# A batch's projections end 6 slots ahead of its scores in place of 24, and the order of tiles, roots, packs and loads around them changes

## The reference, cut to what matters

```python
def _rmsnorm(t):
    return t * jax.lax.rsqrt(jnp.mean(t * t, axis=-1, keepdims=True) + EPS)
q = x @ Wq.T                       # x: layer norm of the block's input
k_raw = context @ Wk.T
v_raw = context @ Wv.T
...
q = _rmsnorm(q)
k = _rmsnorm(k)
scores = jnp.einsum('bhnd,bhmd->bhnm', q, k) * scale
attn = jax.nn.softmax(scores, axis=-1)
out = jnp.einsum('bhnm,bhmd->bhnd', attn, v)
...
x = x + jnp.tanh(g_xattn[0]) * _L0_xattn_ref(_layernorm(x, axis=-1), ctx_2048, L0_xattn_Wq, L0_xattn_Wk, L0_xattn_Wv)
x = x + jnp.tanh(g_ffn[0]) * _L0_ffn_ref(_layernorm(x, axis=-1), L0_ffn_router_w, ...)
```

## Time and profile before

| what | value |
|---|---|
| median of 3 runs | 1108.07 us (1106.4 to 1108.37) |
| the profiled execution: its time | 1103.48 us |
| its span | 1101.4 us |
| TensorE busy | 1047.0 us, 95% of the span |
| VectorE busy | 603.8 us, 55% |
| ScalarE busy | 568.7 us, 52% |
| GpSimd busy | 169.3 us, 15% |
| mean granted clock of TensorE | 0.977 |

### The profile page before, as it was taken

One profiled execution on the slowest core, in us unless ns is written; L12 is line 12 of the kernel. 1 busy time (PEld: TensorE's weight loads), 2 busy tenths in 40 slices (PEclk: granted clock), 3 DMA queues, 4 the chain that ended last, 5 costly groups with the idle time before them and its releaser, 6 DMA issues. The chain is left out here.

```text
span 1101.4 us, 26510 instructions
## 1 busy us (share of the span) xinstructions
PE 1047.0 (95%) x11645; PEld 852.4 (77%) x11645; DVE 603.8 (55%) x1187; ACT 568.7 (52%) x862; POOL 169.3 (15%) x170
## 2 busy tenths in 40 slices
PE   4889999999999999999669999999999999999997
PEld 3667777777777777776458788888888999999996
DVE  4774455644446554553447644434447666666663
ACT  4356766766676676667543221212125555555552
POOL 0000111101111111111322220000011212333111
PEclk9999999999999999999669999999999999999999
DMA  7400000000000000000113120101038777787762
GB/s 231 104 8 29 30 29 29 30 20 11 29 30 29 29 29 29 2 2 2 43 32 126 50 69 20 39 20 36 15 119 247 233 219 232 231 233 221 214 206 77
DMA packets 62170, 93.14 MB, mean 85 GB/s; under 512 B 5378, under 2 KB 43266, under 8 KB 62048
## 3 DMA queue, kind: packets, MB, share of 16 engines
q1 hardware_dynamic: 53544, 74.90, 22.4%
q0 software_dynamic: 5664, 13.18, 3.9%
q10 hardware_dynamic: 2840, 3.29, 1.0%
HBM read 82.24 MB, written 10.29 MB: 84 GB/s over the span
## 5 line engine op out<-in xcount | busy, mean ns | idle before, releaser
L371 PE MATMUL bank<-arena_f32r 128*128 128x512 f32 (+2 forms) x1344 | 367.5, 411 | 16.7 <-DVE arena_f32r L692 16.6
L371 PEld LDWEIGHTS bank<-arena_f32r 128*128 128x128 f32 (+2 forms) x1344 | 228.4, 182 | 76.0 <-DVE arena_f32r L692 11.4
L584 ACT ACTIVATE probs<-score_banks 128x1600 f32<-128x1600 f32 x96 | 144.7, 1507 | 81.6 <-PE score_banks L407 81.6
L1141 ACT ACTIVATE hT_hi<-arena_f 128x224 fp32r<-128x224 f32 (+1 forms) x96 | 42.2, 440 | 165.7 <-DVE arena_f L1148 165.7
L736 POOL TENSOR_TENSOR k_pack<-normed,k_pack 128x512 f16<-128x512 f32 (+1 forms) x45 | 52.5, 1166 | 417.2 <-ACT k_pack L566 417.2
L706 DVE TENSOR_REDUCE sumsq<-arena_f 128x32 f32<-128x512 f32 (+1 forms) x64 | 43.8, 684 | 132.7 <-ACT arena_f L536 132.7
L422 PE MATMUL bank<-probs,values 128*17 128x100 f32 (+1 forms) x3072 | 89.2, 259 | 10.8 <-ACT probs L584 10.8
L422 PEld LDWEIGHTS bank<-probs,values 128*17 128x17 f32 (+1 forms) x3072 | 65.7, 100 | 43.3 <-issue 30.6
L1123 PE MATMUL bank<-arena_f32r 128*128 128x224 f32 (+1 forms) x672 | 93.6, 298 | 0.8 <-DVE heads_out L751 0.8
L1123 PEld LDWEIGHTS bank<-arena_f32r 128*128 128x128 f32 x672 | 91.1, 193 | 2.4 <-DVE heads_out L751 1.2
L1148 DVE TENSOR_TENSOR arena_f<-bank,arena_f 128x224 f32<-128x224 f32 (+1 forms) x96 | 43.1, 449 | 76.1 <-PE bank L1123 76.1
(11 more groups left out here) (176 smaller groups left out, 1819.3 us busy)
## 6 DMA issues: line engine op xcount, KB each, us to landing
arena_f<-L_ffn_w_gate_up SPq DMA_DIRECT2D x32, 512.0 KB, 4.6
w_raw<-L_ffn_w_gate_up SPq DMA_DIRECT2D x32, 512.0 KB, 4.2
arena_f<-ctx SPq DMA_DIRECT2D x15, 722.0 KB, 4.2
w_raw<-L_ffn_w_down SPq DMA_DIRECT2D x16, 512.0 KB, 4.5
arena_f<-L_ffn_w_down SPq DMA_DIRECT2D x16, 512.0 KB, 3.9
x_all<-x SPq DMA_DIRECT2D x4, 800.0 KB
gated_rows<-arena_f POOLq DMA_DIRECT2D x16, 200.0 KB, 3.6
x_rows<-x_all ACTq DMA_DIRECT2D x4, 800.0 KB
```

What stands on the lines that cost most here:

```text
L371: product = PE.matmul(bank[0:rows, :], k.srcT[t % 2][a][:, j, 0:rows], weight, start=(m == 0), stop=(m == 11))
L584: A.activation(k.probs[n % 2][:], k.score_banks[:, :, 0:GH * k.N].rearrange("p j (r n) -> p j r n", r=GH), ACT.Exp, scale=float(HD) ** -0. ...
L1141: A.activation(k.hT[it % 2][0][:, j, 0:width], k.hidden[j][:, 0:width], ACT.Copy).then_inc(r.h_high, 1)
```

## The change

All of it is in attention; the instructions are nearly the same and their order is new.

- `prep_start`: batch b is projected from slot 24 (b - 2) + 18. Its projections end 6 slots ahead of its scores. The loop begins at slot -38 in place of -55 (`k.first_slot`). Projections of the last batch end at slot 354, before at 336. In place of `windows` stand `preparing` and `scoring`; slots of a preparation are counted from `prep_start`, for packs too.
- The products come in the order values 0, keys 0, values 1, keys 1, queries, values 2, keys 2 (`PROJECTION_TILE`, `VALUE_AT`, `HEADS_AT`; `PLACE` and `TILE` give tile 3, the queries, the third place).
- Roots are made in three groups (`RMS_SLOTS`, `RMS_TILES`): keys 0 and 1 on 64 columns, queries on 32, keys 2 on 32. That is 33 small steps a batch in place of 11.
- A batch's first two units wait for four of the five copies, only the third unit waits for the keys of tile 2 (`pe_scores`). Weighted values of tile t wait for that tile's values alone.
- Weighted values stand one slot later (`PV_SLOT` 3), in the slot of the next unit's scores and behind these and the slot's projections. Outputs are turned in slots 14 and 28 in place of 13 and 25.
- All low parts of packs are GpSimd's, the first batch's too.
- x comes in five parts, batch 0 alone and first of all loads (`X_PARTS`, `X_SLOTS`); the query weights come before the second context. Routing moves from slot 355 to 364 (`ROUTE_SLOT`).

```diff
-SRC_SLOTS = (-3, 0, 9, 17)
-WEIGHT_SLOTS = (-55, -48, -47, -47, -40, -39)
-RMS_SLOT = 25
-PACK_SLOTS = (6, 8, 11, 14)
-PACK_T_SLOTS = ((9,), (11,), (15,), (19, 21))
-PV_SLOT = 2
-OUT_SLOTS = (13, 25)
+PLACE = (0, 1, 3, 2)
+TILE = (0, 1, 3, 2)
+VALUE_AT = (0, 2, 5)
+HEADS_AT = (1, 3, 6, 4)
+PROJECTION_TILE = (0, 0, 1, 1, 3, 2, 2)
+SRC_SLOTS = (-3, 0, 6, 13)
+WEIGHT_SLOTS = (-7, 0, 1, 1, 12, 13)
+RMS_SLOTS = (16, 19, 26)
+RMS_TILES = (slice(0, 2), slice(3, 4), slice(2, 3))
+RMS_OF = (0, 0, 2, 1)
+PACK_SLOTS = (18, 19, 28, 21)
+PACK_T_SLOTS = ((22,), (24,), (32,), (26, 27))
+PACK_T_AT = (0, 1, 4, 2)
+PV_SLOT = 3
+OUT_SLOTS = (14, 28)
+X_PARTS = ((0, 1), (1, 4), (4, 8), (8, 12), (12, 16))
+X_SLOTS = (None, -14, 4, 28, 52)
+ROUTE_SLOT = 364
...
+def preparing(k, s):
+    return [(b, s - prep_start(b)) for b in range(k.B) if -4 <= s - prep_start(b) < 40]
+def prep_start(b):
+    return 24 * (b - 2) + LEAD
+def scoring(k, s):
+    return [(b, s - 24 * b) for b in range(k.B) if 0 <= s - 24 * b < 40]
...
 def pe_scores(k, PE, w, s):
-    w.wait_ge(k.kt_copied, 5 * b + 5)
+    w.wait_ge(k.kt_copied, 5 * b + (5 if t == k.NMT - 1 else 4))
 def pe_weighted_values(k, PE, w, b, z, t):
-    w.wait_ge(k.v_copied, 3 * b + 3)
+    w.wait_ge(k.v_copied, 3 * b + t + 1)
...
 def act_source_high(k, A, w, b, t):
-        w.wait_ge(k.projected, 7 * ((n - 2) // 4) + min(2 * ((n - 2) % 4) + 1, 6) + 1)
+        w.wait_ge(k.projected, 7 * ((n - 2) // 4) + HEADS_AT[TILE[(n - 2) % 4]] + 1)
...
-def dve_rms(k, V, w, b):
-    s = k.sumsq[b % 2][:]
-    before = RMS_EVENTS * b
-    w.wait_ge(k.summed, 4 * b + 4)
+def dve_rms(k, V, w, b, g):
+    tiles = RMS_TILES[g]
+    s, root, tmp = (t[:, tiles, :] for t in (k.sumsq[b % 2], k.rms[b % 2], k.rms_tmp))
+    before = RMS_EVENTS * (3 * b + g)
+    w.wait_ge(k.summed, 4 * b + 2 + g)
...
-    k.first_slot, k.last_slot = -55, 24 * k.B + 18
+    k.first_slot, k.last_slot = prep_start(0) - 8, 24 * k.B + 18
```

More of the change, by code:

```diff
@@ L30 @@
 RSQRT_STEPS = 10
-LN_EVENTS = 2 * 4 + 1 + RSQRT_STEPS
 RMS_EVENTS = 1 + RSQRT_STEPS
@@ L279, in turn_order @@
     for s in range(k.first_slot, k.last_slot):
-        for it, i in windows(k, s):
-            order += [("src", it + 2)] if it + 2 < k.B and i == SRC_SLOTS[3] else []
-            order += [("pack", it + 1, t, half) for t in range(4) for half in range(len(PACK_T_SLOTS[t]))
-                      if 0 <= it + 1 < k.B and i == PACK_T_SLOTS[t][half]]
-            order += [("out", it, z) for z in range(2) if it >= 0 and i == OUT_SLOTS[z]]
+        for b, j in preparing(k, s):
+            order += [("src", b)] if j == SRC_SLOTS[2] else []
+            order += [("pack", b, t, half) for t in range(4) for half in range(len(PACK_T_SLOTS[t]))
+                      if j == PACK_T_SLOTS[t][half]]
+        for b, i in scoring(k, s):
+            order += [("out", b, z) for z in range(2) if i == OUT_SLOTS[z]]
     return order, {name: n for n, name in enumerate(order)}
@@ L477, in act_attention @@
-        if s == 354:
+        for b, j in preparing(k, s):
+            for p in range(4):
+                if j == SRC_SLOTS[p] + 1:
+                    act_source_high(k, A, w, b, TILE[p])
+            for n in range(7):
+                if j == taken_slot(n):
+                    if n in VALUE_AT:
+                        act_copy_values(k, A, w, b, PROJECTION_TILE[n])
+                    else:
+                        act_take_heads(k, A, w, b, PROJECTION_TILE[n])
+            for t in range(4):
+                if j == PACK_SLOTS[t] + 1:
+                    act_pack_high(k, A, w, b, t)
+                for half in range(len(PACK_T_SLOTS[t])):
+                    if j == PACK_T_SLOTS[t][half] + 1:
+                        act_copy_pack(k, A, w, b, t, half)
@@ L634, in dve_attention @@
-        for c in range(4):
-            dve_layer_norm(k, V, w, c, 1, s - 96 * (c + 1) - X1_SLOT)
-        if s == 353:
+        for c in range(len(X_PARTS)):
+            if c:
+                dve_layer_norm(k, V, w, 0, c, s - X_SLOTS[c])
+            elif s == k.first_slot:
+                for step in range(CT + 2):
+                    dve_layer_norm(k, V, w, 0, 0, step)
+        for b, j in preparing(k, s):
+            for p in range(4):
+                if j == SRC_SLOTS[p] + 2:
+                    dve_source_low(k, V, w, b, TILE[p])
+            if j == SRC_SLOTS[2] - 2:
+                dve_normalise_x(k, V, w, b)
+            for n in range(7):
+                if j == taken_slot(n) + 1 and n not in VALUE_AT:
+                    dve_sum_squares(k, V, w, b, PROJECTION_TILE[n])
+            for g in range(3):
+                if j == RMS_SLOTS[g]:
+                    dve_rms(k, V, w, b, g)
+            for t in range(4):
+                if j == PACK_SLOTS[t]:
+                    dve_scale(k, V, w, b, t)
```

277 lines of the change are left out of this document (121 added, 156 removed).

## The result

The changed kernel takes 1172.88 us (1170.77 to 1173.49) against 1108.21 us (1106.4 to 1108.37) for the kernel before on the same chip: a ratio of 1.0584, 95% interval [1.0566, 1.0602]. Its profiled execution took 1170.77 us, with a span of 1168.8 us. The forecast was 1180 us, the range 1122 to 1206.

What follows compares the result with a forecast made beforehand. TensorE was taken to bound the steady batches, with idle time only at both ends. Start -11, the 14 batches +80 and end +3 us gave +72 on 1103.48, so 1175.5 profiled and 1180 us forecast, range 1122 to 1206.

Steps and rivals of the forecast that it cites:

- The mechanism: Steady stage: TensorE idles each batch at the second keys' turn, released by ScalarE's copy, clock below 1.00, batch 35 to 38 us.
- The wait: Second keys' turn, every batch: TensorE has 13.5 us of work, the turn comes 3.0 us late.
- The chain: ScalarE and VectorE steps from the second keys' projection to their turn, with GpSimd holding narrow root steps: 16.45 us.
- the rival in which GpSimd holds nothing: Second keys' turn: narrow steps not held, wait 1.85 us, clock stays; 1134 to 1148 us, chance 0.22.
- Fills: TensorE in each batch: three more stretches of projections, each costing a fill, 0.33 us a batch (bounds 0 and 0.9).
- The small terms: Waits per batch: 0.15 us at the next batch's first projection, 0.35 us at the last keys' turn.
- Clock: 14 batches: TensorE's clock falls behind the wait; 20 us taken, half of the upper bound 41, lower bound 0.
- Layer norms: Six of 14 batches: they lengthen the second keys' chain, three by about 1.5 us, three by 2.4; 12 us.
- The start: Up to the first scores: 63 fewer projections, two fewer turns; about 53 us for 63.88, -11 us (bounds -15, -7).
- against it stand new waits: Before the first scores: about 2.3 and 2.6 us at two keys' turns, 5 at the second batch's first projection.
- The end: From the fifteenth batch's first scores: 62.5 us, +3 (bounds -4, +8); router's turn at about 39, then 23 to 25.
- The chain fits: Rival at the second keys' turn: ScalarE and VectorE 3 us faster, TensorE stays the bound; 1094 us, chance 0.11.

Runs made afterwards that it cites:

- source_early: The changed kernel with the next batch's first source high part 3 slots earlier on ScalarE: 1150.27 us, ratio 1.0396.
- copy_early: The changed kernel with that source part 3 slots earlier and the first turned keys' copy ahead of the fifth unit's exponential and queries' pack: 1148.09 us, ratio 1.0386.
- short_low: The changed kernel with GpSimd's low part for the first keys cut to 2 of 32 heads: 1142.29 us, ratio 1.0334.
- fills_alone: The kernel before with only weighted values one slot later and the outputs' turns at 14 and 26: 1111.59 us, ratio 1.0052.

## Why the forecast was right, and where only its sum was

**The mechanism held.** The wait came at the second keys' turn, released by ScalarE's copy to `kT`, behind a stretch of 3.28 us in which ScalarE waited for VectorE. Half clock followed in all but the first batch, and the batch was 37.45 us, in the 35 to 38 forecast. source_early and copy_early show that ScalarE's order makes this wait; short_low shows that the hold on the narrow step feeds it.

**The wait: 1.93 us, not 3.0.** TensorE's side was right: from 249.21, the end of the second keys' projection, to 262.77 it has 13.56 us of work, forecast 13.5. The chain took 15.49 us, forecast 16.45. It was over-sized at two places. From the projection's end to the sum of squares it took 2.19, not 2.65 (249.21 to 251.40). The queries' roots took 3.31, not 3.65: the hold is 0.89 us (1.08 less 0.19), and I had counted a whole part of GpSimd, 1.15, though the step starts inside it. The rest of the chain is within 0.2 us of its terms. The wait measured is nearer to the 1.85 of the rival in which GpSimd holds nothing than to 3.0; that the hold is there all the same is read from the step of 1.08 us and from short_low, where the wait is 1.20.

The Trainium skill ("SBUF — State Buffer", section "Who interferes with whom") has a VectorE instruction with two SBUF inputs contend with a GpSimd one that reads SBUF. The trace agrees for a step of 32 columns: 1.08 us in place of 0.19.

**Fills: 0.93 us a batch, not 0.33.** fills_alone measures this term by itself. I had counted three new stretches of projections; there are six, one in each unit, and a stretch ahead of weighted values costs 0.1 us more than one of the same length ahead of a turn. The earlier trace rows have a like row, four projections ahead of weighted values in 1.10 us; I noted its 0.2 in the bounds and left it out of the sum. My bound of 0.9 us is just passed.

A batch of source_early less its waits, all at full clock, is 35.18 - 1.87 = 33.31 us, against my 32.03 + 0.33 = 32.36. That is 0.4 us more than the parting explains. It lies ahead of the three keys' turns that wait: there three projections take 0.92 us where they take 0.80 ahead of a turn that doesn't wait, seven take 1.86 for 1.73 (fills_alone), and four take 1.17 where they take 1.03 ahead of an output's turn. So a wait costs some 0.13 us more than the view of waits says, and this term I had put at nothing.

**The errors cancel, and that is luck.** An ordinary batch of after is 33.31 + 1.93 + 0.25 + 0.44 + 1.48 = 37.41 us; the forecast has 32.36 + 3.0 + 0.15 + 0.35 + 20 / 14 = 37.29. So +79.4 against +80 owes its closeness to two errors of about a microsecond a batch each, the wait too large and the work too small. Over the stage the 13 other batches make 2 us more than forecast, and the first, 34.48 us where I counted it like the rest, 2.8 less. The small terms were right: 0.25 for 0.15 at the next first projection, 0.44 for 0.35 at the last keys' turn.

**Clock: half of the upper bound, by luck.** I had taken 20 us as an average over batches with and without the fall. The fall is in all batches but the first, at half the loss of the earlier trace rows: 1.48 us in each of the ten with the wait of 1.93, 14.8 us, and more in each of the three long ones, where it is part of their excess.

**Layer norms: 12 us, by another way.** Of the batches with the early ones the second and third are longer by 0.26 us each, not 1.5 (in the first it can't be told apart); the three with finished rows by 3.75, not 2.4. The step that failed is that they lengthen the chain of the second keys. In the three long batches the wait is at the first keys' turn, 4.89 us for the finishing of an output, a queue that the forecast didn't have, and TensorE is at half clock behind it.

**The start: -16.35, not -11, outside my bounds.** Its terms don't give -11 either: -16.4 and -0.8 with 9.9 us of new waits are -7.3, nearer to nothing with a half clock, so -11 is no sum of what is listed. The step that failed is "against it stand new waits". They are there, 2.06 us at the first keys' turn (forecast 2.3), 6.19 at the second (forecast 2.6) and none of the forecast 5 at the second batch's first projection: 8.25 us in all for 9.9. What I left out are old waits that go. In the kernel before, TensorE and VectorE:

```profile
27.70 4.45 PE L371 MATMUL bank<-arena_f32r 128*105 128x512 f32 x12 [5.41 <-DVE arena_f32r L692]
...
46.11 2.83 PE L371 MATMUL bank<-arena_f32r 128*128 128x512 f32 x11 [2.00 <-DVE arena_f32r L692]
```

```profile
19.43 0.69 DVE L673 BATCH_NORM_STATS2 ln_raw<-x_all 100x6 f32<-100x512 f32 x1 [4.16 <-DMA x_all<-x]
...
27.05 0.59 DVE L692 TENSOR_TENSOR arena_f32r<-arena_f,arena_f32r 128x420 fp32r<-128x420 f32 x1
```

VectorE stood 4.16 us for x's first rows, then did statistics of four batches and the queries' weights, and the third source's low part came behind them; TensorE waited 5.41 us for it. In after, with x in smaller parts and the queries fifth, that wait and the 2.00 are gone; no run has either of the two alone, so which of them does it is not shown. Idle time of the stage was 17.6 us and is 17.9; so nearly all that the 63 fewer projections and two fewer turns take, 16.6 us of busy time, is gained. I read the sum of the idle time and not its rows.

**The end: +2.9 for +3.** TensorE came to the router's turn 39.5 us behind the fifteenth batch's first scores (forecast 39), and took 22.6 from there (forecast 23 to 25). Its turn, from the timeline of after:

```profile
620.33 0.59 PE L850 MATMUL bank<-ident,arena_f 8*128 8x8 f32 x4 [2.86 <-DMA arena_f<-L_ffn_router_w]
```

**The rivals.** "The chain fits" fell by 2 us a batch, not by 3. The shorter wait (1.85 us, clock kept) had nearly the size of the wait but not its other half: at 1.93 us the clock fell in 10 of 11 batches. short_low comes near that rival, without the hold and with the clock kept in ordinary batches; but its wait is 1.20 us and its fills are larger, so that its 1142 us lie inside 1134 to 1148 is in part chance.

## What to carry to other kernels

When a step is moved nearer to its use, list every queue that must pass in the shorter time, with what stands ahead of each member: here four engines took turns (ScalarE behind VectorE behind GpSimd, and one PSUM bank that eight turns share), and each run's wait showed which of them came last. Moving one of them alone moved the wait; clearing all of them, with the turns in bank 0 at least two slots apart, gave the early start for nothing. And a saving at the ends of a pipeline is counted once, a wait in its steady stage as often as it has rounds.
